# Gathers of node rows issued in fours behind TensorE's events, 30 warming products, and src rows normalised ahead of the K copies, in a graph attention layer

## What is computed

```python
h = relu(layernorm(x))                               # no gain, no bias
Q, K, V = h @ Wq, h @ Wk, h @ Wv                     # 8 heads of 32
scores = sum over a head of Q[dst] * K[src], times 32 ** -0.5
w = exp(scores - max(0, max over the edges of a dst))
w = w / (sum of w over the edges of a dst + 1e-8)
out = (sum over the edges of a dst of V[src] * w) @ Wo + bo
out = layernorm(h + out) * g1 + b1
out = layernorm(out + gelu(out @ W1 + fb1) @ W2 + fb2) * g2 + b2
result = x + out
```

## Time and profile before

| | us |
|---|---|
| median of 3 runs | 1744.41 |
| lowest and highest | 1738.28, 1752.1 |
| the profiled execution | 1733.5 |
| its span, from the first to the last instruction | 1731.6 |
| mean granted TensorE clock over the span | 0.978 of full |

### The profile page before, as it was taken

How to read it: one execution, slowest core, us unless ns; L and a number is a source line. 1 busy time by engine, 2 the same in 40 slices (tenths; PEclk the granted TensorE clock), 3 DMA queues, 4 the chain that set the end, 5 groups by cost and what they waited for, 6 DMA issues and landing times.

```text
span 1731.6 us, 31120 instructions
## 1 busy us (share of the span) xinstructions
PE 1622.8 (94%) x10389; PEld 1458.0 (84%) x10389; DVE 1513.1 (87%) x4615; ACT 1318.5 (76%) x2419; POOL 1268.1 (73%) x1281
## 2 busy tenths in 40 slices
PE   3887888998888999999999999999999999999997
PEld 2877777875667999999999999999999999999997
DVE  2676677978855999999999999999999999999996
ACT  1565667764465888888888888888888888888884
POOL 6465555426667888888888888888888888888883
PEclk7999899999999999999999999999999999999999
DMA  5588577525426777777777777777777777777761
GB/s 166 207 298 298 197 269 271 175 69 170 116 105 111 176 171 175 169 182 174 177 174 169 179 174 178 177 171 175 167 183 173 179 174 170 178 173 178 175 131 68
DMA packets 95281, 303.92 MB, mean 176 GB/s; under 512 B 16236, under 2 KB 21834, under 8 KB 95120
## 3 DMA queue, kind: packets, MB, share of 16 engines
q0 software_dynamic: 42336, 138.54, 39.8%
q1 hardware_dynamic: 52784, 163.38, 27.1%
HBM read 134.61 MB, written 118.53 MB: 146 GB/s over the span
## 4 chain that ended last, share of the span: by engine, by line
PE 68%; POOL 1%; DMA 0%; DVE 0%; issue 0%; ACT 0%; POOLq 0%; DVEq 0%; ACTq 0%
PE banks L966 32%; PE banks L955 30%; PE banks L941 5%; DMA vt<-agg_scratch 0%; ACT vt L1163 0%; POOL d_zx_rstd L1279 0%; DVE d_y_stats L1081 0%; POOL vt L1264 0%; POOL agg_scratch L1227 0%; DVE d_act_lo L1041 0%; POOLq L1324 0%; POOL vt L1266 0%; DMA agg_scratch<-c_rows,c_row_of 0%; DVE banks L1060 0%; POOL vt L1253 0%
## 5 line engine op out<-in xcount | busy, mean ns | idle before, releaser
L966 PE MATMUL banks<-d_w_hi,d_act_hi 128*128 128x256 f32 x1564 | 457.6, 293 | 0.0
L966 PE MATMUL banks<-d_w_lo,d_act_hi 128*128 128x256 f32 x1564 | 441.9, 283 | 0.0
L966 PE MATMUL banks<-d_w_hi,d_act_lo 128*128 128x256 f32 x1564 | 441.4, 282 | 0.0
L1163 ACT ACTIVATE vt<-vt,d_zx_nmr,d_zx_rstd 128x256 f32<-128x256 f32 x391 | 222.7, 594 | 145.7 <-POOL d_zx_nmr L1282 145.7
L955 PE MATMUL banks<-d_zt_hi,d_w_hi 128*128 128x512 f32 (+1 forms) x784 | 306.2, 391 | 4.6 <-DVE d_zt_lo L1048 2.7
L955 PE MATMUL banks<-d_zt_lo,d_w_hi 128*128 128x512 f32 (+1 forms) x784 | 305.8, 390 | 0.0
L955 PE MATMUL banks<-d_zt_hi,d_w_lo 128*128 128x512 f32 (+1 forms) x784 | 304.9, 389 | 0.0
L966 PEld LDWEIGHTS banks<-d_w_hi,d_act_lo 128*128 128x128 f32 x1564 | 298.8, 191 | 0.0
L966 PEld LDWEIGHTS banks<-d_w_hi,d_act_hi 128*128 128x128 f32 x1564 | 298.4, 191 | 0.1
L966 PEld LDWEIGHTS banks<-d_w_lo,d_act_hi 128*128 128x128 f32 x1564 | 298.0, 191 | 0.0
L1264 POOL TENSOR_TENSOR vt<-vt,d_g_row 128x1024 f32<-128x1024 f32 x98 | 288.7, 2946 | 2.9 <-ACT vt L1163 2.9
(11 more groups left out here) (167 smaller groups left out, 3606.4 us busy)
## 6 DMA issues: line engine op xcount, KB each, us to landing
agg_scratch<-vt SPq DMA_DIRECT2D x100, 512.0 KB
vt<-in_x SPq DMA_DIRECT2D x97, 512.0 KB
vt<-agg_scratch POOLq DMA_DIRECT2D x97, 512.0 KB, 5.5
vt<-vt POOLq DMA_DIRECT2D x97, 512.0 KB, 7.5
out<-vt SPq DMA_DIRECT2D x97, 512.0 KB, 2.9
a_xd<-in_x,a_idx POOLq DMA_INDIRECT x98
a_xs<-in_x,a_idx POOLq DMA_INDIRECT x98
score_scratch<-a_score SPq DMA_DIRECT2D x98, 4.0 KB
```

What stands on the lines that cost most here:

```text
L966: ins = nc.tensor.matmul(Y[s % 2][:, j, :], a[:, c, j * P:(j + 1) * P], w[:, c, :], start=False, stop=(c == KF - 1 and w is w2_lo), skip_g ...
L1163: ins = nc.scalar.activation(zn[gz % 2][:, j, :], z[gz % ZR][:, j, :], ACT.Identity, bias=zx_nmr[:, at % NR, 0, j:j + 1], scale=zx_rstd[:, ...
```

## The change

It does four things. `WARM` goes from 70 to 30. GpSimd's gathers get other waits: in the start, src of group 1 and everything of groups 2 and 3 now wait for an event of TensorE each; from group 4 on, dst of g waits for the first half of Q(g - 3) and src of g for the first half of V(g - 3). ScalarE normalises the first two src rows of group s + 1 ahead of the first key copy of step s and the other two between the two key copies, where all four stood behind the dst high part. VectorE's order in steps -1 and 0 is other: the low parts come ahead of the statistics of the next group's src (and in step 0 of the dst too).

```diff
-    WARM, IDLE = 70, 18
+    WARM, IDLE = 30, 18
@@ gpsimd
+                    if g == 1 and n == GT:
+                        pool.wait_ge(t_done[0], 1)
+                    elif g == 2 and n == 0:
+                        pool.wait_ge(q_done, 1)
+                    elif g == 2 and n == GT:
+                        pool.wait_ge(k_done, 2)
+                    elif g == 3 and n == 0:
+                        pool.wait_ge(v_done, 1)
+                    elif g == 3 and n == GT:
+                        pool.wait_ge(t_done[1], 2)
+                    elif g > XG and n == 0:
+                        pool.wait_ge(q_done, 2 * (g - XG) + 1)
+                    elif g > XG and n == GT:
+                        pool.wait_ge(v_done, KD * (g - XG) + 1)
                     if g >= XG and j == 0:
                         pool.wait_ge(h_done[side], g + 1 - XG)
-                    if g >= XG + 1 and n == 0:
-                        pool.wait_ge(v_done, KD * (g - XG - 1) + 1)
-                    if g >= XG and n == GT:
-                        pool.wait_ge(q_done, 2 * (g - XG) + 1)
@@ vector
                 elif s == -1:
                     low_part(0, 0)
+                    low_part(0, 1)
                     statistics(1, (1,))
-                    low_part(0, 1)
                     inverse_root(1)
+                elif s == 0:
+                    products(0)
+                    low_part(1, 0)
+                    head_sums(0)
                     statistics(2, (0,))
+                    low_part(1, 1)
+                    statistics(2, (1,))
+                    inverse_root(2)
+                    statistics(3, (0,))
@@ scalar
             for s in range(FIRST, EG):
+                if 0 <= s < AHEAD:
+                    normalise(s + 1, 1, (0, 1))
                 key_copy(s, 0)
-                if s == -1 or s >= AHEAD:
+                if s >= -1:
                     normalise(s + 1, 1, (2, 3))
                 key_copy(s, 1)
                 high_part(s + 1, 0)
-                if 0 <= s < AHEAD:
-                    normalise(s + 1, 1, (0, 1, 2, 3))
```

## The result

The changed kernel takes 1712.97 us, median of five executions (1708.79 to 1714.69); the kernel before, on the same chip, 1738.34 (1737.55 to 1752.10). The ratio is 0.982, with a 95% interval of 0.980 to 0.985: 1.8% faster, 27 to 35 us; the two medians lie 25.4 us apart. The forecast was 1723, which is 1.2% under its base.

A forecast was written before the change was run, and what follows sets the result against it. TensorE carried 68% of the chain, with warming products holding the start for about 22 us. The terms 21.1 - 1.2 - 1.3 - 2 + 4 = 20.6 us, off the 1744.4 median, gave 1723; range 1702 to 1744.

The forecast's parts named there:

- part 1: Start: with 30 warming products instead of 70, step 0's first product starts near 27.3 instead of 48.43, 21.1 us gained.
- rival A: Start: the starving is not the gathers', step 0 starts near 45, gain 0 to 4 us, about 1740; chance 0.20.
- part 2: Steps 0 and 1: first gathers behind events cost 1.2 and 1.3 us, delayed TensorE events 2 us more.
- The worry over the clock: Step 0: with less warming it might run at 1.2 GHz; taken as 0, with 5 us kept for the range.
- part 3: Later gathers, half a step later: no more instructions or idle time for GpSimd, 0; lead shrinks but stays covered by 3.6 us.
- part 4: Middle steps: src rows ahead of the key copies gain 4 us, between -6 and +12.
- B: Score stage: src rows' reordering pays in full and the clock dips go, 29 us gained, 1715; chance 0.12.
- C: Steps filling the scratch table: gathers land too late and delay VectorE; 1764 at 2 us a step; chance 0.08.
- D: Tight steps: ScalarE is the path and the src rows' reordering gives -6 us, 1734; chance 0.10.

The follow-up runs named there:

- experiment 6: The kernel before with 30 warming products and the scratch table's fill of steps 0 and 1 moved into step 2; 1736.91 us in one execution.
- experiment 5: The changed kernel with 70 warming products again; 1708.86 us, ratio 0.985 to the kernel before.
- experiment 1: The kernel before with 30 warming products instead of 70 and nothing else; 1735.97 us, ratio 1.000.
- experiment 8: The changed kernel with group 4's dst gathers waiting for the end of K(1) instead of Q(1); 1707.54 us, ratio 0.984 to the kernel before.
- experiments 2: The changed kernel with the gathers from group 4 on at their old events and ScalarE's old order; 1721.03 us, ratio 0.993 to the kernel before.
- experiment 4: The changed kernel with ScalarE's old order, src rows behind the dst high part; 1713.75 us, ratio 0.988 to the kernel before.
- experiment 9: The kernel before with only GpSimd's two waits swapped, TensorE's ahead of the one for `h_done`; 1723.20 us, ratio 0.992.
- experiment 10: The changed kernel with GpSimd's `h_done` wait put back ahead of TensorE's from the fourth group on; 1736.81 us, ratio 0.999 to the kernel before.
- experiment 3: The kernel before with ScalarE's new order of the src rows alone; 1747.23 us, ratio 1.007.
- experiment 7: The changed kernel with the gathers from group 4 on at their old events, ScalarE's order still new; 1711.82 us, ratio 0.987 to the kernel before.

## Why the prediction was right or wrong

**The start (part 1): right, in size and in reason.** Q(0) at 26.8 against 27.3. The starving belonged to the gathers, as the prediction chose against its rival A: experiment 6 shows it without the fill, and in experiment 5 it is gone with the long row, though the fill is there. The rule of the Trainium skill (page "SBUF — State Buffer", section "Who interferes with whom") that PE never waits on anyone stands there among rules on SBUF's ports, and the prediction read it more widely. Read so, it would have kept the stretch where it was; the trace has the event of finished transposes held for 19 us (experiment 1). But the prediction booked the 21 us under the warming. Experiments 1 and 5 show that they belong to part 2, the waits of the first groups: thirty products without those waits are worth nothing, and seventy products with them cost nothing. The worry over the clock is not borne out: with seventy products it stays at 1.00 and Q(2) starts 3.6 us earlier than in after, but experiment 8 has thirty, and its step 0 takes 14.0 us beside 13.8 with seventy. After's 17.2 goes with its row of eight.

**Steps 0 and 1 (part 2): the cause was named, the size was wrong.** The terms were 1.2, 1.3 and 2 us, and the measured loss is 11.1: step 0 went from 13.4 to 17.2 and step 1 from 13.6 to 20.9. The failed term is the last one, "GpSimd is then behind and issues five runs nearly back to back, which delays TensorE's events; I take 2 us, between 0 and 5". Eight gathers from 29.17 and twelve from 41.53 ran in a row. The same prediction held that a row of 28 starves TensorE and a row of four doesn't, and did not ask where twelve would fall. They fall on the side of the 28: the event of K(1)'s first half is held for 10 us and ScalarE idle for 6.27. What such a row costs is shown by experiments 2 and 4, where sixteen in place of twelve make step 1 6.3 us longer. No run with the new start has less than twelve there, so the price of the twelve themselves is not measured.

**The middle steps (parts 3 and 4): right in direction, wrong in cause.** The sum had +4 for the src rows and 0 for GpSimd. The src rows gave 3.5 us in the middle steps, experiment 4 against after, near the 4 that were taken; but by the medians they gave nothing that these runs can tell, so the agreement is in one pair of traces. The step that failed is in part 3, "no more instructions and no new idle time for GpSimd, 0". It looked at which event each four waits for and how long the lead is, and not at the order in which the two waits stand, which the diff changes as well. That order alone gives 9.0 us in the middle steps (285.9 to 276.9, experiment 9) and 12.7 us by the medians; taken out of after, it costs all of the gain (experiment 10). With before's order the src rows cost 13 us by the medians (experiment 3), so the gain that the prediction gave to part 4 holds only behind a change that it did not see. The 0 of part 3 overlooked a second thing: the new place of group 4's dst gathers keeps the row in step 1 at twelve, 7.3 us by the medians of experiments 2 and 4.

**The base.** That the sum came out at 20.6 against 20.4 is luck: two of its terms are wrong and cancel. Between the profiled executions the gain is 20.4 us, as summed, between the medians 25.4, and by the ratio 27 to 35. The prediction put a sum made from the profiled execution, 1733.5, onto a median of three that lay 10.9 higher. The table's last column shows what it passed over: with `h_done` first the executions scatter over 17 to 22 us, with TensorE's wait first over 2 to 7. The profiled execution of before was quicker than all five timed ones (1737.55 at the least), and the change took most of the scatter away as well. I take it that other executions of before have more fours that run on; no trace of a slower one was taken, so this part is argued.

**The rivals.** A (the stretch stays) fell with Q(0). B had the right order of size, 29 us, but for clock dips and a part 4 in full. The clock in the middle steps is in fact 1.00 where it was 0.95, and 0.97 in the same stretch of experiment 4, without the src rows; what that gave was not separated. C (a lead that is too short) did not occur: between 27 and 345 us of after VectorE waits for a landing once, for 1.8 us, and turning the lead back changes nothing in the middle steps (experiment 7). D's shift in the tight steps did not decide anything.

What stays open: why the kernel of experiment 10, with every part of the change but the swap, has steps of 13.63 rather than 13.0. It has the most fours that run on; why later places make more of them was not separated from the src rows, which alone have ten. That experiments 5 and 8 don't add up was not followed further. Whether a row holds events by GpSimd's issuing or by the traffic of its DMAs was not separated, and VectorE's new order was not run alone.

## What to carry to other kernels

Where an engine issues long rows of gathers, ask for every event of TensorE that falls into a row whether someone is waiting for it, and keep such rows short by a wait for exactly that event. When a gather has two waits, find out which rides on it and which stands ahead as an instruction of its own, and put the one that will be met last on the gather; here that is the one written first. A diff that swaps two waits has changed the schedule, however harmless it looks. When a sum agrees with the result, still compare it line by line: here misses of 6.6 and 8.4 us hid behind a total that was right to 0.2.

## What was unexpected in the hardware

- While a row of indirect gathers runs on GpSimd, TensorE's semaphore events are held back, mostly until behind its last gather, and the longer the row, the later: 1.0 to 1.4 us behind the fours of after's middle steps, 1.7 behind the eight of before at 142.17, 2.5 behind the twelve of after at 56.20, 4.3 behind the long row of experiment 1 at 38.16. In rows of eight and more, over all traces, 111 of the 130 events whose work finished in the first 5 us of the row came out within 0.3 us; of the 59 whose work finished more than 7 us into it, 6 came out ahead of its end.
- Late in such a row TensorE's own issue slows, in after to one instruction per 1.4 to 2.1 us from 50.12 to 58.66, so that it looks like an engine with slow work.
- Two waits ahead of a gather are not alike: 0.26 us from the event to the gather for the one written first, which rides on it, 0.76 for the other, which is an instruction of its own.
- With the order of these two waits goes how far executions of the same kernel scatter, 17 to 22 us against 2 to 7.
